# A flag ahead of the values, a selector copy behind the first queries, and a new order of steps

## Time and profile before

| what | value |
| --- | --- |
| time, median of 3 runs | 1010.57 us (1010.32 to 1011.88) |
| profiled execution, own time | 1010.12 us |
| its span, first to last instruction | 1008.3 us |
| TensorE busy | 952.9 us (94%) |
| ScalarE busy | 805.3 us (80%) |
| VectorE busy | 716.2 us (71%) |
| GpSimd busy | 353.0 us (35%) |
| mean granted TensorE clock | 0.99 |

### The profile page before, as it was taken

The page is one execution under the profiler, slowest core; times in us unless marked ns, Lnnn a source line. Parts: engine busy times, 40 slices in busy tenths (PEclk is TensorE's granted clock), DMA queues, the critical chain, the costliest instruction groups (busy, mean ns, idle before and its releaser), DMA issues.

```text
span 1008.3 us, 16668 instructions
## 1 busy us (share of the span) xinstructions
PE 952.9 (94%) x5863; PEld 457.9 (45%) x5863; DVE 716.2 (71%) x1263; ACT 805.3 (80%) x1052; POOL 353.0 (35%) x311
## 2 busy tenths in 40 slices
PE   4999998999999999999999999999999999999998
PEld 2232245333533453345334523543357666555666
DVE  4243761765787788898897788779799999897300
ACT  2999985899899979999998999989975585644632
POOL 2000121213432554264425331553644565555100
PEclk8999998999999999999999999999999999999999
DMA  7873343183235522662375147423241423341020
GB/s 169 201 200 82 106 121 91 35 207 97 53 112 142 137 64 79 174 151 72 98 167 126 33 121 181 119 66 93 76 135 40 118 64 94 90 140 53 25 59 21
DMA packets 141158, 106.26 MB, mean 105 GB/s; under 512 B 92880, under 2 KB 108272, under 8 KB 141040
## 3 DMA queue, kind: packets, MB, share of 16 engines
q1 hardware_dynamic: 137632, 103.56, 39.6%
q10 hardware_dynamic: 3408, 1.09, 0.4%
HBM read 75.25 MB, written 29.36 MB: 104 GB/s over the span
## 4 chain that ended last, share of the span: by engine, by line
PE 58%; ACT 13%; DVE 12%; issue 9%; DMA 5%; POOL 2%; ACTq 0%; SPq 0%; DVEq 0%; POOLq 0%
PE PS L1546 18%; PE PS L1509 10%; PE PS L1593 10%; ACT R L956 8%; PE PS L1720 5%; PE PS L1708 5%; DVE R L1322 4%; DVE R L1313 3%; DMA R<-VD 3%; PE PS L1655 3%; PE PS L1664 2%; PE PS L1633 2%; ACT L916 2%; DVE RB L1278 1%; PE PS L1448 1%
## 5 line engine op out<-in xcount | busy, mean ns | idle before, releaser
L956 ACT ACTIVATE R<-PS 128x1024 f32<-128x1024 f32 x512 | 488.2, 1035 | 42.3 <-PE PS L1509 38.2
L1546 PE MATMUL PS<-R 128*32 128x512 f32 x2048 | 291.6, 609 | 2.0 <-issue 1.6
L887 POOL TENSOR_TENSOR R<-R 128x512 f32<-128x512 f32 x128 | 186.5, 1462 | 190.1 <-ACT R L1032 132.8
L1509 PE MATMUL PS<-RA 32*128 32x512 f32 x1024 | 181.0, 499 | 27.5 <-ACT R L956 15.6
L1322 DVE TENSOR_TENSOR_SCAN R<-R 128x512 f32<-128x512 f32 x128 | 197.5, 1543 | 2.5
L1509 PEld LDWEIGHTS PS<-RA 32*128 32x128 f32 x1024 | 71.5, 183 | 242.3 <-ACT R L956 156.6
L1593 PE MATMUL PS<-RB,WR 128*128 128x512 f32 x640 | 170.2, 412 | 1.4 <-DVE flags L1193 1.1
L1593 PEld LDWEIGHTS PS<-RB,WR 128*128 128x128 f32 x640 | 116.5, 190 | 61.3 <-issue 31.0
L1313 DVE TENSOR_TENSOR R<-R 128x512 f32<-128x512 f32 x128 | 111.2, 869 | 27.5 <-DMA R<-VD 26.6
L873 POOL TENSOR_TENSOR RB<-R,RB 128x512 fp32r<-128x512 f32 x48 | 72.0, 1501 | 151.0 <-DVE RB L1278 151.0
L916 ACT ACT_TABLE_LOAD x76 | 97.5, 1283 | 30.7 <-PE PS L1593 12.0
(11 more groups left out here) (129 smaller groups left out, 852.9 us busy)
## 6 DMA issues: line engine op xcount, KB each, us to landing
R<-VD SPq DMA_DIRECT2D x128, 256.0 KB, 4.1
RA<-QD SPq DMA_DIRECT2D x64, 256.0 KB, 4.5
QD<-RA SPq DMA_DIRECT2D x56, 256.0 KB, 4.3
OD<-R SPq DMA_DIRECT2D x32, 256.0 KB, 2.1
RA<-QD SPq DMA_DIRECT2D x62, 128.0 KB, 4.1
R<-OD SPq DMA_DIRECT2D x128, 32.0 KB, 2.5
R<-in_Wa SPq DMA_DIRECT2D x12, 256.0 KB, 3.4
R<-in_Wb SPq DMA_DIRECT2D x12, 256.0 KB, 3.9
```

The source lines that it names most:

```text
L887: pool.tensor_tensor(st, st, Qc, ALU.mult).then_inc(S["qh"], 1)
L956: act.activation(PR[u % 4], bank(2 * s, 1024), ACT.Exp, scale=SC).then_inc(S["exp"], 1)
L1509: op = pe.matmul(bank(2 * s + h), exact(KS[k][p:p + 32, 128 * j:128 * j + 128]), exact(QS[k][p:p + 32, :]), start=True, stop=stop)
L1546: op = pe.matmul(bank(ob)[c:c + 32, :], VAF[b % 2][:, at:at + 32], PR[u % 4][:, 512 * h:512 * h + 512], start=(j == 0), stop=(j == 7), til ...
```

## The change

The wait for `gsel` and the copy into GSEL go behind ScalarE's two query loads of `first_pair`. In the head of the plan, `flag` for block 0 stands ahead of `values` for block 0, on every engine. `ORDER` is another string of the same 1812 letters, each letter as often as before.

```diff
@@ ORDER
-    "xxxxxxxxxxxxqxxwxqxxqxxxxqxxxxxxwxxwxxxlxxfwxxxwqxxxxxxxxxwxwqxxlxxwxxxqxlqwxxxxxfxxxlwxxxwwfxxpxxxx"
...
+    "wqxqxqxxxxxxxxxxxxxxxxxxxxxqxxxxxxxxxxwxlxxxxxwqxxwfwxxxxxxxxqxxxxwxxxqlxxxlxwxqfxxlwxwxxwxfwxxpxxxf"
...
@@ Plan.start
         self.add("first_pair", 0)
+        self.add("flag", 0, 2)
         self.add("values", 0, 1)
-        self.add("flag", 0, 2)
@@ ScalarE
             act.activation(epsc[:, 1:2], epsc[:, 0:1], ACT.Exp)
-            need.wait_ge("ones", 17)
-            act.activation(GSEL[:, :], gsel[:, :], ACT.Copy).then_inc(S["ones"], 1)
...
                     queries(act, 0, 0, "pair_in0")
+                    need.wait_ge("ones", 17)
+                    act.activation(GSEL[:, :], gsel[:, :], ACT.Copy).then_inc(S["ones"], 1)
```

More of the change, by code:

```diff
@@ L41 @@
-    "srsrsssdbsbssdbbddstssrdrdtbdssddsrbsdtsrsddpsssspdtsdstsrpsddsdrddstsdpdssddrptpddrdstsssdtpsdssrsd"
-    "tsrddsdrtssddsrdsdssdsssddsztzrdstssdrrstdssrdszdtdssdssdddsdsrrsdssdstrddddsddddsssrsddtssssrrdssst"
-    "ssdddddsdsddtdstddtdddttdddddttdddtdddtddtdtttdttddzdddddzddddtdzddddddddddddddddddddddddddddddddddd"
+    "wqxqxqxxxxxxxxxxxxxxxxxxxxxqxxxxxxxxxxwxlxxxxxwqxxwfwxxxxxxxxqxxxxwxxxqlxxxlxwxqfxxlwxwxxwxfwxxpxxxf"
+    "xxxxxwwxxaxxxwxxwxaawlaxxwwxxxxxxwxqxxxfxawawqwxxxxxxxxwxawxbxfxbxxbbxbxbxxqbxxqxxbbxxqqxbxxxbbllbbb"
@@ new lines @@
+    "bxbxbblxqxbbfxxbxbfxxxxxaxbaxxbxxaxapqxxxpxaxrqxparlqpqxpaxpxbfxsqsrxbxbxxbxpxxrsxqrxxxxbxfxssxsxxxs"
+    "ssxxxxssxxxxxxsxrsbxbxbsbfsxlsqxxssxbrsbrbxbxsrxblblbxrbsxbssfsbssxsabsssbxxxbxsxrrxbrxsxbsxxraxaxxs"
+    "sxsxxaslxaxbssfxxassxpxxsssxrabpsxqxxsbxxsrqxxsxbsbrxpqpxppsrqsxxqxsxlbbxxsbxbxpxxbbsbbbxxxssslxrfxx"
+    "xxsxxsxrxsxxsrtqsrsfsxsxbsblssbbsxxtsxrsrrtxsbfqbssxsxsxbrbxbxxsxxxxssbxasxssxbsxralbxsxsatxaxrspxsq"
+    "xxxtxsrrssxsxsxxxxaxxxaqsxxasbpxsxxsxrrqrbxsqpfssxbqpxssxrxxbxxxslptpbxssxsbxptfsxxxbbsxssrxxxqsxxlr"
@@ new lines @@
+    "xblstsxsfqrbrssbbxbxsbsbstbbfssxtsxsbbrtxsrbssrbassxtssxxsbxxasbxarsxxxxssxxxxbsxrarxxtsaxbsrxqassxx"
+    "pxsplxatxqxrxbxssssxxsxqxqspxtsbxxbxsxxxtxxrtrqlxpxbrstxxlxsbbtxqssfxxxsbxtxpxstpxxbsxrsstbxxspsxqsl"
+    "stxrsfxsbtxxbbbbbrbbfxsxtrfxbxxssabsbbsxtsbxxsrbaxxsssasxrxxxsrxsxssxrxxxatxxssxsxbsxrxsassxsqsabrrs"
+    "xxsprxpsxsssslqrxxsaxbsxxsxssxsxrpxrqrxfxssrsqbxpxsxqxxsqsxbtxtpxbxxpsxxbltfssxxxftsplxxbxbxlbbssxsx"
+    "rtxbbbtbxrsxbsbbtbxxxssbsbtrfxarbbsssxsxxbbsxtxssxsbxrxrarbsxsssxtppxsxrsstasxxsxssxasaxxxpsrtxxsrrx"
@@ new lines @@
+    "sxsfsxlrxssssxstsxxxsxsxfxaxsrtxxartxsxrsrtbxsxxxsspxbxxxptpxxsbstbsxxsbbxsxpfxbssbxxbsxrxsszbbsbrbb"
+    "bztbbsfsdrdbrsaszbssbbasdstatsbtsdbtzdrdasadstdsrtrsddsrssbdsdddssdssddstrddasdrdsssdbrabsdzrddddtsd"
+    "tdsbdsddssbbsbptsdbsdbrrbpdsrbssdssppdrppssbsspsbsddsdsdbrdsztsrsdbtdrsdssbsdbsrdbstbddsdststsbbrrbr"
+    "ssbssddssrtsssbbssdsstrdstsdrsbdrddbsdssddtsssdpprsssdddsrdptrstdpdsddrsrtsdsspptddddssssddsdpssrttr"
+    "sstddsdsdddtrsdssdssrddsztsdssrdsrsdrddttszzsdsddssrdtdsddsdsdssdstdrdtdsdsrdsrdtsdssdrssssdssdsrsrs"
@@ L44 @@
+    "sssddssdtddddddsdtdddttdtdddtddtdtdddtdddttdttttztdddzddddddzddddddddddddddddddddddddddddddddddddddd"
     "dddddddddddd"
```

## The result

The changed kernel takes 1021.65 us (median of 4 runs, 1020.97 to 1024.04), the kernel before 1011.23 us beside it (4 runs, 1010.32 to 1013.02). The ratio is 1.0105, 95% interval 1.0082 to 1.0128: 10.6 us slower by the ratio, where 5.3 us faster was forecast. The profiled execution has a span of 1019.1 us against 1008.3.

A forecast was written before the change was run, and what follows sets the result against it. TensorE's work plus its 55.4 us idle time was taken as the bound. Terms -0.3 - 6.0 - 0.8 + 0.8 + 0.5 + 0.5 = -5.3 us gave 1005.3 us, range 1000.0 to 1013.0 for 8 in 10.

The forecast's parts named there:

- The rest of the order: Remaining places of the new order: 37.7 us of TensorE's idle time dealt anew, taken as zero, 4 us either way.
- Guard(2): Hole of 4.67 us at 157.39 us plus 2.2 us low clock: all but 0.9 us gained, -6.0 us.
- The lower bound of this term: At the 157 us hole: 3.02 us pause and low clock stay, 5.2 us, so only 0.8 us is gained.
- The first queries: Start: line 937 near 7.3 us, first scores 1.4 us earlier, third exponential 0.65 us later; -0.3 us for the start.
- fifth exponential: Start of attention: the fifth exponential begins 0.65 us later to 0.25 us earlier than before.
- Guard(6): Pause of 1.58 us in the weighing behind this guard: half taken as gained, -0.8 us (-1.6 to 0).
- guard(3): Two hid_mm ahead of this guard in place of three, less to cover a pause: +0.5 us (0 to 3.02).
- project(1): Waited 0.8 us for divide(1), loses the pair of weigh ahead of it: +0.8 us (0 to 4).
- route_1: Third batch: stands behind its turn_c by four products in place of seven: +0.5 us (0 to 1.3).
- third rival: Slower: the pause moves to other guards, two hit by 4.67 us each; 1014.6 us, chance 0.17.
- last sign: Forecast wrong as a whole if TensorE's idle time falls under 2 us though the hole at 157 us is gone.
- second rival: The hole at 157 us stays, or ScalarE later limits attention; 1010.5 us, no change, chance 0.19.

The follow-up runs named there:

- e3: The new order alone, with the head of the kernel before; 1.0077 of the kernel before.
- e9: The kernel before without TensorE's four skipped pieces of each guard's path, flag still loaded; 0.988 of the kernel before, median 999.88 us.
- e10: The changed kernel without TensorE's four skipped pieces of each guard's path, flag still loaded; 1.0016 of the kernel before, median 1013.35 us.
- e5: The changed kernel's head and order up to the 272nd x (piece of attention scores), the old order behind; 0.9984 of the kernel before.
- e6: The kernel before up to the 272nd x (piece of attention scores), the new order behind; 1.0123 of the kernel before.
- e4: The kernel before with ten more loads of the table already in use, ahead of exponentials; 1.0152 of the kernel before.
- e7: The kernel before with Tanh for Gelu in the ternary net's two hidden levels, 38 table loads left of 76; 0.9978 of the kernel before.
- e13: The kernel before with the new order's sequence between the 272nd and 330th x (pieces of attention scores); 1.0058 of the kernel before.
- e14: The kernel before with the new order from the 430th x (piece of attention scores) on; 1.0135 of the kernel before.
- e11: The kernel before with one letter q moved ten places forward, so flag(2) comes earlier; 1006.88 us, 0.9949 of the kernel before.
- e12: The kernel before with flag(2) ten places earlier and the GSEL copy behind the query loads; 1006.2 us, 0.9937 of the kernel before.

## Why the prediction was wrong

**The step that failed** is the last of the sum: "The rest of the order ... All other places change as well. Of the 55.4 us idle, 13.0 lie ahead of the first scores and 4.7 in the hole; the other 37.7 are dealt anew. I take zero for that, and a tenth of it, 4 us, either way." With the head left as it was, the order costs 0.77% (e3), 7.8 us, and without the pauses at the guards the change costs 1.38%, 13.5 us (e9, e10). Not only the size but the reason for zero failed: idle time dealt anew was taken as a draw, and busy time as fixed. In place of zero the runs show 7.8 to 13.5 us, all of it that can be seen behind the 272nd x (e5, e6). Part of it is seen in the traces: in the old order TensorE's matmuls seldom waited for what VectorE and GpSimd make, in the new one they often do (14.8 against 32.7 us), and over half of the longer span is busy time that the sum had no term for. That these waits are the cause is argued, not shown: most of their growth is made up by shorter waits for ScalarE and DMA, and in e13 and e14 the time grew without them or by more than they did. The prediction works out four places and leaves the rest of the 1812 letters. Nor does it count the table loads, which follow from the order alone, 86 against 76; as e4 and e7 show, that count would have been a warning and no price.

**Guard(2)** was mis-sized. I took 6.0 us gained, all of the hole but 0.88. The part due to the late flag went, the fetch stayed at 2.12 us, and 3.25 us with a low clock appeared at guard(5): the sum of pauses at guards is 7.4 before and 7.1 after. The lower bound of this term had a slip as well: keeping 5.2 of 6.9 us gains 1.7, not 0.8. What was right is the reading of the second part of the hole as code not being there (e9: with the jumped-over pieces gone, no pause). What was wrong is that a pause seen once would not come back: guards 2 and 5 of the changed kernel, 2 of e11 and 2 of e12 all have one of 2.1 to 3.3 us. The Trainium skill (Runtime: NRT & Kernel Launch, Instruction fetch mechanics) says that a branch to code outside the loaded window forces a fetch first; e9 and e10 agree, and I had set this aside because guard(1) has only 0.88 us.

**The first queries** were right, point by point, from line 937 to the third exponential, each within 0.4 us, and so was the reason that they bring nothing: VectorE's list sets scores(2) in the new order. In e3, without the head's edits, scores(2) even starts 0.6 us sooner. The fifth exponential came 0.2 us later than the latest that was forecast for it.

**Guard(6), guard(3), project(1), route_1**: no pause is marked at guards 3 and 6 (forecast +0.5 and -0.8, in fact 0 and -1.6); TensorE no longer waits for the division at line 1201 (+0.8 forecast, in fact the 0.8 us of the earlier trace rows are gone); route_1 waits twice, 2.1 us in all, for 1.3 (+0.5 forecast). None of them matters beside 10.6 us.

**The rivals and the signs.** The third rival, slower by moved pauses, had the direction and named the mechanism of the pause at guard(5), one guard for the two it counted; but e9 and e10 show that pauses aren't what made the whole change slower, so the time went its way for another cause. The prediction's last sign came true in substance: most of the hole went, and TensorE's idle time did not fall but grew by 4.8 us. The second rival was right in its first half, a pause stays at guard(2); its second half, ScalarE as what later limits attention, is not borne out: TensorE's scores wait 11.2 us for exponentials in the changed kernel and 15.6 in the one before, and 38 loads fewer change little.

```profile
PE PS L1509 <- ACT R L956: 15.6, 50, 0.8
```

```profile
PE PS L1509 <- ACT R L956: 11.2, 40, 0.4
```

The first row is the kernel before, the second the changed one (matmuls waiting for line 956: us in all, times, longest).

**Where the 10.6 us lie.** From the matmul starts, at equal amount of matmul work, the changed kernel is behind by +0.4 us at 121 us, ahead by 4.0 from 174 to 275, ahead by 1.5 at 374, then behind: +3.0 at 424, +7.8 at 471 (guard(5) is in it), +5.5 up to 671, +11.9 at 815, +10.7 at the end (own calculation from the two traces). Guard(2) did give 4 us; behind 374 us it lost 12.2 us (from -1.5 to +10.7). Which waits behind 374 us make it up stays open.

## What to carry to other kernels

A new order of steps is not one edit that pays at the hole it was made for: all waits are dealt anew, and here the rest of the order cost more than the hole. Zero for that rest needs a reason of its own. A first look costs nothing: count from the order, for each result that the busiest engine reads, what stands ahead of its producer in the producer's own list (that this count would have given the price is not shown). Don't take the wait that grew most for the cause before a run in which the time moves and the wait doesn't has been looked for; e13 was one. A pause behind a jump has two parts, the value that the branch needs and the code it lands on; moving the value earlier takes away only the first. And moving one letter (e11) gained what the whole new order didn't.

## What was not expected of the hardware

A table load lasts 1283 ns in every trace here, but its price goes from 1.56 us each (e4, ten ahead of exponentials, 15.6 us) to about 0.06 us each (e7, 38 loads for 2.2 us): where it stands decides. My reading, not tested further: ahead of an exponential TensorE soon waits for it (its waits for ScalarE are 31.5 us in e4 and 23.1 in the kernel before), elsewhere ScalarE has room.

Code that never runs cost 12 us of 1012 (e9): four pieces jumped over at each of eight guards. In the changed kernel the pause is 2.12 and 3.25 us at two guards and 0.9 us or less at the others, and it moved from guard to guard with the order of steps around it.
